# An LSTM's new cell moves from PSUM to SBUF, its forget gate from SBUF to PSUM

## The chip, the cores and the metric

One NeuronCore of one Trainium2 chip. The metric is the device time of one execution in microseconds; lower is better.

## What is computed

Sixteen sequences of 128 steps with 128 features pass through two LSTM layers that follow each other: the first feeds an attention without softmax, the second a feed-forward block, each with a residual. The recurrence is what matters here:

```
def step(carry, xp_t):
    prev_h, prev_c = carry
    h_bar = xp_t + prev_h @ Wh
    i = sigmoid(h_bar[:, 0:H]);      f = sigmoid(h_bar[:, H:2*H])
    o = sigmoid(h_bar[:, 2*H:3*H]);  g = tanh(h_bar[:, 3*H:4*H])
    next_c = f * prev_c + i * g
    next_h = o * tanh(next_c)
...
x = x + attn(lstm1(x, cond), W_theta, W_phi, W_g)    # attn: (theta phi^T / sqrt(128)) g
x = x + relu(lstm2(x, cond) @ W1 + b1) @ W2 + b2
```

The hidden size H is 128, so `Wh` is 128 x 512. There are 2 x 128 = 256 steps, each needs the one before it, and the second layer can't begin before the first has ended.

## The kernel before

The hidden state lies transposed, features on the 128 partitions and the 16 batch rows as columns, so that everything in a step is 128 x 16. `ring` keeps h of 16 steps in fp32; `h_hi` and `h_lo` keep it split into two fp16 numbers. A layer is cut into chunks of 8 steps (`CH`); ITER loops of 16 steps (`STEPS`) run over a layer. The first loop and, for layer 1, the last are written out, the others are hardware loops.

Each engine runs its own list in order, and the engines are tied together by semaphores set by hand. In a step:

- TensorE (`step`, L408): waits for `ring` and multiplies it by `whf`, the forget gate's fp32 weights (L420), into `fbank`; then `h_hi` and `h_lo` by the fp16 weights of g and i (L414) into `gibank`, then by those of o into `bankV`. After that it does what stands beside the step (`beside1` for layer 1: projections, attention, transposes; feed-forward products and projections for layer 2) and filler matmuls (`keep_warm`, L389, and `add_zeros`, L400), some of which wait for the o gate's sigmoid.
- ScalarE (ACT, L787): forget sigmoid from `fbank` to `fgate` (L795); one tanh for i and g together, from `gibank` into slots of `scan` (L802; sigmoid is had from tanh of the half, which is why the cell is kept at a doubled scale); o's sigmoid to `ogate` (L806); the tanh of the new cell to `tanhc` (L809). Copies such as `seed_o` (L825) stand between steps.
- VectorE (DVE, L983): the forget product `fgate` times old cell into every third column of `scan` (L987); `tensor_tensor_scan` over 48 columns (L990), which does the multiply and add for each of 16 batch rows in three columns and leaves the new cell in each third column; `ogate_h` (L995); `ring`, the new h in fp32 (L998), `h_hi` (L1000) and `h_lo` (L1003).

`cell` is a PSUM bank. Its first 48 columns are the scan's output `c_scan`, the next 16 are `tanhc`; `c_psum` is every third column of `c_scan`. `fgate`, `ogate`, `ogate_h` and `scan` are in SBUF. At the very end the bank `cell` also takes one product of the feed-forward block.

Of the kernel before, what the change touches and what calls it, by code (L numbers as in the profile page):

```python
# [30 lines left out]
def build(nc, x, cond, l1_wx, l1_wh, l1_b, w_theta, w_phi, w_g,  # L31
# [5 lines left out]
    ACT = mybir.ActivationFunctionType  # L37

    NB, T, D = x.shape
    H = D  # L40
    LAT = w_theta.shape[0]
    P = 128
# [19 lines left out]
    with ctx:  # L62
        def sb(name, shape, dt=f32):
            return ctx.enter_context(nc.sbuf_tensor(name, shape, dt))

        def ps(name):
            return ctx.enter_context(nc.psum_tensor(name, [P, 512], f32))

        def sem(name):
            return ctx.enter_context(nc.semaphore(name))  # L70
# [34 lines left out]
        w2 = sb("w2", [P, NJ, D])  # L105
        b1 = sb("b1", [P, NJ])
        b2 = sb("b2", [P, D])
        fgate = sb("fgate", [P, NB])
        ogate = sb("ogate", [P, NB])
        scan = sb("scan", [P, 98])  # L110

        h_hi = sb("h_hi", [P, STEPS, NB], f16)
        h_lo = sb("h_lo", [P, STEPS, NB], f16)
# [25 lines left out]
        fbank = [ps("fbank0"), ps("fbank1")]  # L139
        cell = ps("cell")  # L140
        bankU, bankV, bankY = ps("bankU"), ps("bankV"), ps("bankY")
        c_scan, tanhc = cell[:, 0:3 * NB], cell[:, 3 * NB:4 * NB]
        c_psum = c_scan.rearrange("p (b k) -> p b k", k=3)[:, :, 2]
        scan_mul, scan_add = scan[:, 0:3 * NB], scan[:, 3 * NB + 1:6 * NB + 1]
        gi_slots = scan[:, 2:6 * NB + 2].rearrange("p (g b k) -> p g b k", g=2, k=3)[:, :, :, 0]
        fc_slots = scan_add.rearrange("p (b k) -> p b k", k=3)[:, :, 2]
# [39 lines left out]
        hi_ready = [sem("hi_ready1"), sem("hi_ready2")]  # L186
# [60 lines left out]
        def rest_of_first(g):  # L247

            nc.vector.scalar_tensor_tensor(out=part(0, 1, g), in0=wh[0][:, gate_cols(g)], scalar=w_unit(0),
                                           in1=part(0, 0, g), op0=ALU.mult, op1=ALU.subtract  # L250
                                           ).then_inc(parts_ready[0], 1)
# [489 lines left out]
        def _(act):  # L741
# [9 lines left out]
            def high_parts(layer):  # L751

                nc.scalar.mul(wh_parts[layer][:, 0, :], wh[layer][:], w_unit(layer)).then_inc(parts_ready[layer], 1)
# [33 lines left out]
            def step(layer, s, n, first=False, opening=False):  # L787

                p, t = s // CH, s % CH
                n1 = n + 1  # L790
                if opening:
                    act.sem_inc(f_done[layer], 1)
                else:
                    act.wait_ge(f_ready[layer], n1)
                    nc.scalar.activation(fgate[:], fbank[p][:, NB * t:NB * t + NB],  # L795
                                         ACT.Sigmoid, scale=1.0 / Z_UNIT).then_inc(f_done[layer], 1)
                if first:
                    act.wait_ge(wh_ready, 1)
                    act.wait_ge(scale_made[0], SCALED - 2)
                    high_parts(0)  # L800
                act.wait_ge(gi_ready[layer], n1)
                nc.scalar.activation(gi_slots,  # L802
                                     gibank[p][:, 2 * NB * t:2 * NB * (t + 1)].rearrange("p (g b) -> p g b", g=2),
                                     ACT.Tanh, scale=0.5 / Z_UNIT).then_inc(scan_inputs[layer], 1)
                act.wait_ge(o_ready[layer], n1)
                nc.scalar.activation(ogate[:], bankV[:, (2 + p) * P + NB * t:(2 + p) * P + NB * t + NB],  # L806
                                     ACT.Sigmoid, scale=1.0 / Z_UNIT).then_inc(o_done[layer], 1)
                act.wait_ge(c_ready[layer], n1)
                nc.scalar.activation(tanhc, c_psum, ACT.Tanh,  # L809
                                     scale=0.5).then_inc(h_inputs[layer], 1)  # L810

            def keep_rows(slot, i, c, bank=bankY):
# [38 lines left out]
            for s in range(STEPS):  # L851
                step(0, s, s, first=s == 0, opening=s == 0)
                beside1(0, s, first=True)
                if s < 2:
                    keep_proj(s)
                set_layer2(s)
            with act.Fori(1, ITER - 1) as i:
                for s in range(STEPS):
                    step(0, s, i * STEPS + s)
                    beside1(i, s)  # L860
            for s in range(STEPS):
                step(0, s, (ITER - 1) * STEPS + s)
                beside1(ITER - 1, s, last=s >= CH)
# [29 lines left out]
        def _(dve):  # L893
# [89 lines left out]
            def step(layer, s, n, first=False, opening=False):  # L983
                n1 = n + 1
                if not opening:
                    dve.wait_ge(f_done[layer], n1)
                    nc.vector.tensor_tensor(out=fc_slots, in0=fgate[:], in1=c_psum,  # L987
                                            op=ALU.mult).then_inc(scan_inputs[layer], 1)
                dve.wait_ge(scan_inputs[layer], n * 2 + 2)
                nc.vector.tensor_tensor_scan(out=c_scan, data0=scan_mul, data1=scan_add, initial=0.0,  # L990
                                             op0=ALU.mult, op1=ALU.add).then_inc(c_ready[layer], 1)
                if first:
                    rest_of_first(GI)
                dve.wait_ge(o_done[layer], n1)
                nc.vector.tensor_tensor(out=ogate_h[:], in0=ogate[:], in1=unit_fill[layer][:],  # L995
                                        op=ALU.mult).then_inc(h_inputs[layer], 1)
                dve.wait_ge(h_inputs[layer], n * 2 + 2)
                nc.vector.tensor_tensor(out=ring[:, s, :], in0=tanhc, in1=ogate_h[:],  # L998
                                        op=ALU.mult).then_inc(h_ready[layer], 1)
                nc.vector.tensor_tensor(out=h_hi[:, s, :], in0=tanhc, in1=ogate_h[:],  # L1000
                                        op=ALU.mult).then_inc(hi_ready[layer], 1)
                dve.wait_ge(hi_ready[layer], n1)
                nc.vector.tensor_tensor(out=h_lo[:, s, :], in0=ring[:, s, :], in1=h_hi[:, s, :],  # L1003
                                        op=ALU.subtract).then_inc(lo_ready[layer], 1)
                if first:
                    rest_of_first(GO)
# [34 lines left out]
            for s in range(STEPS):  # L1041
                step(0, s, s, first=s == 0, opening=s == 0)
                beside1(0, s)
                if s == 1:
                    most_of(w_halves[:, 0:1], slice(0, 2 * H), 1, wh2_loaded)
                if s == 2:
                    most_of(w_halves[:, 1:2], slice(2 * H, 4 * H), 1, wh2_loaded)
                if s == 3:
                    dve.wait_ge(scale_made[1], 2)
                    nc.vector.tensor_reduce(w_most[1][:], w_halves[:], axis=mybir.AxisListType.X, op=ALU.max  # L1050
                                            ).then_inc(scale_made[1], 1)
                    spread_most(1, 3)
                if s == 4:
                    top_of(1, bankU[:, 2 * P:3 * P])
                if s == 6:
                    power_of(1, 5)
                if s == 7:
                    inverse_of(1, 7)
                if s == 8:
                    units_of(1, 8)  # L1060
                if s == 9:
                    fills_of(1, 10)
                if s == 14:
                    rest_of_second(slice(0, H))
                if s == 15:
                    rest_of_second(slice(2 * H, 4 * H))
            with dve.Fori(1, ITER) as i:
                for s in range(STEPS):
                    step(0, s, i * STEPS + s)
                    beside1(i, s)  # L1070
# [48 lines left out]
            with dve.Fori(1, ITER) as i:  # L1119
                for s in range(STEPS):  # L1120
                    p, t = s // CH, s % CH
# [44 lines left out]
```

## Time and profile before

| | |
|---|---|
| median of 3 runs | 435.31 us (435.3 to 435.46) |
| span of the profiled execution | 431.1 us |
| PE, matmul | 413.9 us busy, 96% |
| PE, weight load | 301.4 us, 70% |
| DVE | 282.0 us, 65% |
| ACT | 192.1 us, 45% |
| granted TensorE clock | full through the whole span |

The profiled execution's own time isn't given apart from its span; the median of the runs lies 4.2 us above the span. PE is busy time of matmuls, whose ends are modelled since they are pipelined, and PEld is the weight load that overlaps them. A high busy share of an engine doesn't say that the engine sets the time: the waits, and the timeline of one step, do.

### The profile page before, as it was taken

The page shows a single profiled execution, that of the slowest core. Times are in us where ns is not written, and L with a number is a line of the kernel's source. Part 1 is how long each engine was busy: PE and PEld are TensorE (multiplying, and loading weights), DVE is VectorE, ACT ScalarE, POOL GpSimd, SP SyncE. Part 2 cuts the span into 40 slices and gives each one's busy share as a digit, 9 for nine tenths or more (in the row PEclk, how much of TensorE's full clock was granted, in tenths as well). Part 3 has the DMA queues.
Part 4 walks back from the last instruction along what each step waited for, and adds up shares of the span by engine and source line. Part 5 has one row for each costly group of instructions (what it writes and reads, how often), then busy time and mean ns, then how long its engine had stood idle before and what let it go on. Part 6 is the DMA issues. An engine that isn't in the chain of part 4 may idle for free.

```text
span 431.1 us, 14329 instructions
## 1 busy us (share of the span) xinstructions
PE 413.9 (96%) x5020; PEld 301.4 (70%) x5020; DVE 282.0 (65%) x1702; ACT 192.1 (45%) x1132; POOL 7.8 (2%) x20
## 2 busy tenths in 40 slices
PE   8999999999999999999999999999999999999996
PEld 5767666666766666666689777777777777777775
DVE  6766666666666666666668766666667666666664
ACT  3565444445444444544445433343443434343342
POOL 7000000000000000000000000000000000000000
PEclk9999999999999999999999999999999999999999
DMA  5011011111001111000000100000000000000000
GB/s 180 10 20 20 13 10 18 18 18 18 13 5 18 18 18 18 16 2 14 14 14 2 27 21 6 12 18 20 18 18 0 18 18 18 18 17 1 18 18 12
DMA packets 11694, 8.19 MB, mean 19 GB/s; under 512 B 1097, under 2 KB 11129, under 8 KB 11674
## 3 DMA queue, kind: packets, MB, share of 16 engines
q1 hardware_dynamic: 10874, 6.17, 7.2%
q0 software_dynamic: 512, 1.22, 0.9%
q10 hardware_dynamic: 288, 0.52, 0.4%
q8 instruction: 13, 0.21, 0.2%
q14 instruction: 7, 0.06, 0.0%
HBM read 2.87 MB, written 1.05 MB: 9 GB/s over the span
## 4 chain that ended last, share of the span: by engine, by line
PE 83%; ACT 7%; DVE 5%; issue 3%; DMA 1%; SPq 0%; DVEq 0%
PE fbank L420 19%; PE bankV L400 14%; PE gibank L414 9%; PE bankU L389 6%; PE bankV L414 5%; PE gibank L377 4%; PE bankY L619 4%; PE bankU L612 3%; DVE cell L990 3%; PE bankV L484 3%; ACT scan L802 3%; PE bankY L479 2%; ACT fgate L795 2%; PE gibank L383 2%; PE bankU L512 2%
## 5 line engine op out<-in xcount | busy, mean ns | idle before, releaser
L420 PEld LDWEIGHTS fbank<-ring,whf 128*128 128x128 f32 x508 | 76.6, 188 | 91.7 <-DVE ring L998 88.1
L795 ACT ACTIVATE fgate<-fbank 128x16 f32<-128x16 f32 x254 | 46.5, 183 | 153.5 <-PE fbank L420 153.2
L420 PE MATMUL fbank<-ring,whf 128*128 128x16 f32 x508 | 98.2, 269 | 6.1 <-DVE ring L998 0.7
L987 DVE TENSOR_TENSOR scan<-fgate,cell 128x16 f32<-128x16 f32 x254 | 45.1, 178 | 77.5 <-ACT fgate L795 75.4
L400 PE MATMUL bankV<-warm_x,zeros 128*128 128x512 bf16 x294 | 93.0, 379 | 0.0
L990 DVE TENSOR_TENSOR_SCAN cell<-scan 128x48 f32<-128x48 f32 x256 | 68.2, 267 | 12.0 <-ACT scan L802 1.1
L809 ACT ACTIVATE cell<-cell 128x16 f32<-128x16 f32 x256 | 43.0, 168 | 67.9 <-DVE cell L990 67.8
L998 DVE TENSOR_TENSOR ring<-cell,ogate_h 128x16 f32<-128x16 f32 x256 | 44.7, 174 | 41.8 <-ACT cell L809 41.6
L414 PEld LDWEIGHTS gibank<-h_hi,wh_parts 128*128 128x128 f16 x1016 | 65.4, 117 | 0.0
L414 PE MATMUL gibank<-h_hi,wh_parts 128*128 128x16 f16 x1016 | 62.1, 169 | 0.0
L414 PE MATMUL gibank<-h_lo,wh_parts 128*128 128x16 f16 x1016 | 62.0, 169 | 0.0
L802 ACT ACTIVATE scan<-gibank 128x32 f32<-128x32 f32 x256 | 54.5, 213 | 4.2 <-PE gibank L383 1.6
L1003 DVE TENSOR_TENSOR h_lo<-ring,h_hi 128x16 f16<-128x16 f32 x256 | 44.9, 175 | 8.7
L414 PE MATMUL bankV<-h_hi,wh_parts 128*128 128x16 f16 x508 | 49.3, 169 | 0.0
L414 PE MATMUL bankV<-h_lo,wh_parts 128*128 128x16 f16 x508 | 49.3, 169 | 0.0
L806 ACT ACTIVATE ogate<-bankV 128x16 f32<-128x16 f32 x256 | 46.9, 183 | 0.0
L414 PEld LDWEIGHTS gibank<-h_lo,wh_parts 128*128 128x128 f16 x1016 | 43.4, 96 | 0.0
L1000 DVE TENSOR_TENSOR h_hi<-cell,ogate_h 128x16 f16<-128x16 f32 x256 | 42.1, 165 | 0.0
L995 DVE TENSOR_TENSOR ogate_h<-ogate,unit_fill 128x16 f32<-128x16 f32 x256 | 41.5, 162 | 0.0
L389 PE MATMUL bankU<-warm_x,warm_w 128*128 128x512 bf16 x128 | 37.9, 377 | 0.0
L400 PEld LDWEIGHTS bankV<-warm_x,zeros 128*128 128x128 bf16 x294 | 29.0, 99 | 8.7
L414 PEld LDWEIGHTS bankV<-h_lo,wh_parts 128*128 128x128 f16 x508 | 30.6, 96 | 0.0
(182 smaller groups left out, 505.6 us busy)
## 6 DMA issues: line engine op xcount, KB each, us to landing
rows_t<-rows SPq DMA_DIRECT2D x16, 128.0 KB
x_rows<-in_x_dram SPq DMA_DIRECT2D x17, 64.0 KB
out_dram<-y_sb SPq DMA_DIRECT2D x16, 64.0 KB
xres<-x2T SPq DMA_DIRECT2D x15, 64.0 KB, 1.9
xin<-x2T SPq DMA_DIRECT2D x14, 64.0 KB, 1.9
w<-in_L_ffn_W_dram POOLq DMA_DIRECT2D x2, 256.0 KB, 4.1
wh<-in_L_cond_Wh_dram ACTq DMA_DIRECT2D x1, 256.0 KB, 2.7
wx<-in_L_cond_Wx_dram ACTq DMA_DIRECT2D x1, 256.0 KB, 3.6
```

The lines of the kernel that those rows point to most:

```text
L389: nc.tensor.matmul(bank[:, :], warm_w[:], warm_x[:], start=True, stop=True)
L400: nc.tensor.matmul(bankV[:, :], zeros[:, 0:P], warm_x[:], start=False, stop=True, skip_group_check=True)
L414: last = nc.tensor.matmul(step_out(p, t, g), wh_parts[layer][:, part, gate_cols(g)], h[:, (s - 1) % STEPS, :], start=False, stop=True, ski ...
L420: nc.tensor.matmul(step_out(p, t, GF), whf[layer][:], ring[:, (s - 1) % STEPS, :], start=False, stop=True, skip_group_check=True).then_inc ...
L795: nc.scalar.activation(fgate[:], fbank[p][:, NB * t:NB * t + NB], ACT.Sigmoid, scale=1.0 / Z_UNIT).then_inc(f_done[layer], 1)
L802: nc.scalar.activation(gi_slots, gibank[p][:, 2 * NB * t:2 * NB * (t + 1)].rearrange("p (g b) -> p g b", g=2), ACT.Tanh, scale=0.5 / Z_UNI ...
L806: nc.scalar.activation(ogate[:], bankV[:, (2 + p) * P + NB * t:(2 + p) * P + NB * t + NB], ACT.Sigmoid, scale=1.0 / Z_UNIT).then_inc(o_don ...
L809: nc.scalar.activation(tanhc, c_psum, ACT.Tanh, scale=0.5).then_inc(h_inputs[layer], 1)
L987: nc.vector.tensor_tensor(out=fc_slots, in0=fgate[:], in1=c_psum, op=ALU.mult).then_inc(scan_inputs[layer], 1)
L990: nc.vector.tensor_tensor_scan(out=c_scan, data0=scan_mul, data1=scan_add, initial=0.0, op0=ALU.mult, op1=ALU.add).then_inc(c_ready[layer], 1)
L998: nc.vector.tensor_tensor(out=ring[:, s, :], in0=tanhc, in1=ogate_h[:], op=ALU.mult).then_inc(h_ready[layer], 1)
L1003: nc.vector.tensor_tensor(out=h_lo[:, s, :], in0=ring[:, s, :], in1=h_hi[:, s, :], op=ALU.subtract).then_inc(lo_ready[layer], 1)
```

## The change

The scan's output `c_scan` becomes an SBUF tensor of its own, [128, 48] in fp32; the new cell, every third column of it, is called `c_new`. `fgate` leaves SBUF and takes the first 16 columns of the PSUM bank `cell`; `tanhc` follows it in columns 16 to 31. The instructions are the same, in the same order. ACT gets one wait more: before the forget sigmoid of step n it waits until `hi_ready` has reached n, which is when DVE has made `h_hi` of the step before, the last reader of `tanhc` in the bank that the sigmoid now writes.

```diff
-        fgate = sb("fgate", [P, NB])
         ogate = sb("ogate", [P, NB])
         scan = sb("scan", [P, 98])
+        c_scan = sb("c_scan", [P, 3 * NB])
...
-        c_scan, tanhc = cell[:, 0:3 * NB], cell[:, 3 * NB:4 * NB]
-        c_psum = c_scan.rearrange("p (b k) -> p b k", k=3)[:, :, 2]
+        fgate, tanhc = cell[:, 0:NB], cell[:, NB:2 * NB]
+        c_new = c_scan[:].rearrange("p (b k) -> p b k", k=3)[:, :, 2]
...
                 else:
+                    act.wait_ge(hi_ready[layer], n)
                     act.wait_ge(f_ready[layer], n1)
-                    nc.scalar.activation(fgate[:], fbank[p][:, NB * t:NB * t + NB],
+                    nc.scalar.activation(fgate, fbank[p][:, NB * t:NB * t + NB],
                                          ACT.Sigmoid, scale=1.0 / Z_UNIT).then_inc(f_done[layer], 1)
...
-                nc.scalar.activation(tanhc, c_psum, ACT.Tanh,
+                nc.scalar.activation(tanhc, c_new, ACT.Tanh,
                                      scale=0.5).then_inc(h_inputs[layer], 1)
...
-                    nc.vector.tensor_tensor(out=fc_slots, in0=fgate[:], in1=c_psum,
+                    nc.vector.tensor_tensor(out=fc_slots, in0=fgate, in1=c_new,
                                             op=ALU.mult).then_inc(scan_inputs[layer], 1)
                 dve.wait_ge(scan_inputs[layer], n * 2 + 2)
-                nc.vector.tensor_tensor_scan(out=c_scan, data0=scan_mul, data1=scan_add, initial=0.0,
+                nc.vector.tensor_tensor_scan(out=c_scan[:], data0=scan_mul, data1=scan_add, initial=0.0,
                                              op0=ALU.mult, op1=ALU.add).then_inc(c_ready[layer], 1)
```

## Rows read from the trace of the kernel before

**Rows 1.** The page: busy time by engine, and the chain that ended last

```profile
PE 413.9 (96%) x5020; PEld 301.4 (70%) x5020; DVE 282.0 (65%) x1702; ACT 192.1 (45%) x1132; POOL 7.8 (2%) x20
...
PE 83%; ACT 7%; DVE 5%; issue 3%; DMA 1%; SPq 0%; DVEq 0%
```

**Rows 2.** Waits: engine and line, for whom; us in total, times, longest

```profile
PEld fbank L420 <- DVE ring L998: 88.1, 226, 0.5
```

**Rows 3.** Timeline, one step of layer 1: start us, length us, instruction

```profile
105.86 0.38 PE L400 MATMUL bankV<-warm_x,zeros 128*128 128x512 bf16 x1
105.95 0.17 DVE L998 TENSOR_TENSOR ring<-cell,ogate_h 128x16 f32<-128x16 f32 x1 [0.16 <-ACT cell L809]
106.05 0.17 DVE L1000 TENSOR_TENSOR h_hi<-cell,ogate_h 128x16 f16<-128x16 f32 x1
106.18 0.30 PEld L420 LDWEIGHTS fbank<-ring,whf 128*128 128x128 f32 x2 [0.44 <-DVE ring L998]
...
106.61 0.18 ACT L795 ACTIVATE fgate<-fbank 128x16 f32<-128x16 f32 x1 [0.69 <-PE fbank L420]
...
106.81 0.21 ACT L802 ACTIVATE scan<-gibank 128x32 f32<-128x32 f32 x1
106.83 0.18 DVE L987 TENSOR_TENSOR scan<-fgate,cell 128x16 f32<-128x16 f32 x1 [0.41 <-ACT fgate L795]
...
107.05 0.27 DVE L990 TENSOR_TENSOR_SCAN cell<-scan 128x48 f32<-128x48 f32 x1
...
107.23 0.16 DVE L995 TENSOR_TENSOR ogate_h<-ogate,unit_fill 128x16 f32<-128x16 f32 x1
107.35 0.17 ACT L809 ACTIVATE cell<-cell 128x16 f32<-128x16 f32 x1 [0.26 <-DVE cell L990]
...
107.55 0.17 DVE L998 TENSOR_TENSOR ring<-cell,ogate_h 128x16 f32<-128x16 f32 x1 [0.16 <-ACT cell L809]
```

**Rows 4.** Groups by line and form, ACT: busy us, mean ns | idle before

```profile
L802 ACT ACTIVATE scan<-gibank 128x32 f32<-128x32 f32 x256 | 54.5, 213 | 4.2 <-PE gibank L383 1.6
...
L795 ACT ACTIVATE fgate<-fbank 128x16 f32<-128x16 f32 x254 | 46.5, 183 | 153.5 <-PE fbank L420 153.2
L809 ACT ACTIVATE cell<-cell 128x16 f32<-128x16 f32 x256 | 43.0, 168 | 67.9 <-DVE cell L990 67.8
L825 ACT COPY bankV<-o_bias 128x128 f32<-128x128 f32 x31 | 8.2, 264 | 0.0
...
L839 ACT ACTIVATE xT<-bankU 128x128 f32 x12 | 3.3, 277 | 0.2
...
L771 ACT ACTIVATE wx<-wx 128x128 f32<-128x128 f32 x1 | 0.3, 302 | 0.0
...
L821 ACT COPY o_bias<-bankV 128x128 f32<-128x128 f32 x1 | 0.3, 265 | 0.2 <-PE bankV L377 0.2
```

**Rows 5.** Timeline of ACT, second step of layer 1, sigmoid held up

```profile
12.00 0.20 ACT L795 ACTIVATE fgate<-fbank 128x16 f32<-128x16 f32 x1
12.09 0.21 ACT L802 ACTIVATE scan<-gibank 128x32 f32<-128x32 f32 x1
```

**Rows 6.** Groups by line and form, DVE

```profile
L990 DVE TENSOR_TENSOR_SCAN cell<-scan 128x48 f32<-128x48 f32 x256 | 68.2, 267 | 12.0 <-ACT scan L802 1.1
...
L1003 DVE TENSOR_TENSOR h_lo<-ring,h_hi 128x16 f16<-128x16 f32 x256 | 44.9, 175 | 8.7
L998 DVE TENSOR_TENSOR ring<-cell,ogate_h 128x16 f32<-128x16 f32 x256 | 44.7, 174 | 41.8 <-ACT cell L809 41.6
...
L995 DVE TENSOR_TENSOR ogate_h<-ogate,unit_fill 128x16 f32<-128x16 f32 x256 | 41.5, 162 | 0.0
...
L1135 DVE TENSOR_TENSOR y_sb<-bankY,b 128x128 f32<-128x128 f32 x14 | 4.0, 287 | 0.0
```

**Rows 7.** Timeline, a step of layer 2 with late TensorE: filler, sigmoid

```profile
307.18 0.81 PE L400 MATMUL bankV<-warm_x,zeros 128*128 128x512 bf16 x3
...
308.15 0.18 ACT L795 ACTIVATE fgate<-fbank 128x16 f32<-128x16 f32 x1 [0.93 <-PE fbank L420]
```

## The prediction

> **What bounds the kernel now.** I read the busy shares first. TensorE shows 96% of the span, and the chain that ended last gives PE 83% [rows 1], which looks like a kernel bound by TensorE. It isn't: much of that work is filler (the products of `warm_x`), and the wait list says who waits for whom. The weight load of the forget gate's matmul sat idle for DVE's `ring` 226 times, 88.1 us in all, 0.39 us a time [rows 2]. So in 226 of the 256 steps TensorE has caught up and waits for the recurrence.
>
> Next the timeline of one step [rows 3]. From `ring` at 105.95 to the next at 107.55 is 1.60 us, and 256 steps of it are 410 of the 431.1 us of the span. Its links, start to start: `ring` to the load of `whf` 0.23, to the forget sigmoid 0.43, to the i/g tanh 0.20, to the scan 0.24, to the cell tanh 0.30, to `ring` 0.20. A nanosecond on one of these links in every step is worth about 0.23 us.
>
> **What changes in a step.** Four instructions get other operands: the forget sigmoid writes PSUM, the forget product (L987) has `fgate` as its PSUM operand and no longer the cell, the scan writes SBUF, the cell tanh reads SBUF. ACT gets one more wait. No DMA and no matmul is touched.
>
> **Forget sigmoid: worth nothing.** On ACT the write to PSUM is the cheaper one: the sigmoid to SBUF is 183 ns, the cell tanh, PSUM to PSUM at the same width, 168 [rows 4]. The sigmoid should fall by 15 ns, or by up to 25 (the tanh has a stride, below). But nobody waits for it last. The i/g tanh starts 0.20 us after it [rows 3], and could start sooner: in a step where its input had long been there it started 0.09 us after the sigmoid, at 12.09 after 12.00 [rows 5]. In the ordinary step TensorE's i/g products set its start. The product L987 does follow the sigmoid, but it ends at 106.83 + 0.18 = 107.01, the i/g tanh at 106.81 + 0.213 = 107.023, and the scan starts 0.027 later [rows 3, 4]. So the i/g tanh is last, and the sigmoid's gain is hidden behind it: 0. It can't turn into a cost, since the product only gets more lead.
>
> **Forget product: 0.** It had one operand in PSUM and has one after, so its 0.18 us [rows 3] should stay. A growth of some ns is covered by its earlier start.
>
> **Cell tanh: +24 ns, on the path.** SBUF to PSUM at this width isn't in the trace. Two ways lead to it. First, wide activations: PSUM to SBUF is 277 ns (L839), SBUF to SBUF 302 (L771) [rows 4], so reading SBUF costs 25 more; 168 + 25 = 193. Second, wide copies: SBUF to PSUM (L825) is 264, PSUM to SBUF (L821) 265 [rows 4], so the direction makes no difference and the tanh would cost what the sigmoid costs, 183. But this one reads with a stride of three. The i/g tanh writes with that stride: 213 ns for 32 elements, where 183 + 16 x 0.84 = 196 would be due (0.84 = (277 - 183)/112 [rows 4]), so the stride costs some 0.5 ns an element, 8 ns for 16; 183 + 8 = 191. I take 192, +24. Bounds: +15 (stride free) and +38 (each strided read costs a second element's time, 25 + 13). Below zero it can't go unless SBUF is read faster than PSUM, and 302 against 277 excludes that.
>
> **Scan: -12 ns, on the path.** No DVE instruction but the scan writes PSUM. The nearest row is the price of reading PSUM: `ring`, with one PSUM operand, is 174 ns, `ogate_h`, the same product all in SBUF, 162 [rows 6]. That is 12 ns for the crossing, and I take the write to cost the same; on ACT, read and write cost alike (264 against 265). The bounds come from splitting its 267 ns [rows 6]. An element costs DVE 1.0 ns ((287 - 174)/112, `y_sb` against `ring`), so an all-SBUF product has a fixed part of 146 (`ogate_h`: 162 - 16) to 159 ns (`h_lo`: 175 - 16) [rows 6]. If the scan takes one such time an element, 48 ns, 219 are fixed and the write to PSUM costs 60 to 73. If it takes two (a multiply and an add that need the last result), 171 are fixed and the write costs 12 to 25. At the other end the write costs nothing. I take 12: the nearest row, and the low end of the two-time case.
>
> The Trainium skill says (DVE: opcode table, instruction layouts, handler registers and perf-mode slots, section Datapath and trigger behaviour) that the built-in scan runs at half throughput, which is the two-time case; no row here shows it. By that page the write would cost 12 to 25 ns and the sum would still end at slower or about the same.
>
> **The added wait: 0.** ACT now waits for `hi_ready` of the step before, ahead of `f_ready`. Behind it on ACT are the forget sigmoid and the rest of that step's activations. `h_hi` ends at 106.05 + 0.17 = 106.22 and the sigmoid starts at 106.61 [rows 3]: 0.39 us of cover, in which ACT is idle. Without that cover each nanosecond would count 226 times.
>
> **Sum.** 24 - 12 = 12 ns a step. It counts in the 226 steps in which TensorE waits for `ring`; in the other 30 something else is late and takes 12 ns without notice. 226 x 12 = 2.7 us: the span goes from 431.1 to 433.8. The median of the runs, 435.31, lies 4.2 above the profiled span; with the same 4.2 the time is 438.0 us.
>
> **The rivals.**
> (a) The forecast, slower by 0.2 to 1% (net +4 to +19 ns): 438.0 us. For it: the ACT price rests on two ways that agree within 2 ns. Against it: the scan's price is borrowed from a read. Chance 0.47.
> (b) Faster: the scan's write to PSUM is dear, 60 to 73 ns. Net -36 to -49, times 226 is -8.1 to -11.1 us, so 425.7 us. The sign turns as soon as the write costs more than the tanh's 24. Nothing would be in the way of such a gain: `ogate_h` ends at 107.39, 0.16 us before `ring` starts, and the filler ahead of the forget matmul ends at 106.24, 0.37 before the sigmoid [rows 3], where elsewhere a filler that ended at 307.99 let the sigmoid start 0.16 later [rows 7]. Against it: reading PSUM costs DVE only 12 ns. Chance 0.16. A mild form, write 28 to 39 ns, gives 431.9 to 434.4 us; chance 0.06.
> The Trainium skill leans to this side (VectorE: DVE Perf Modes, section on the TRN2 errata): it gives VectorE a fixed 58 cycles with an SBUF source and 120 with a PSUM source, ScalarE 224 and 172. Carried over to this swap, -65 and +43 ns a step would be an estimate of about 430 us. The trace disagrees on both sizes for reads, 12 and 25 ns.
> (c) The two cancel within 4 ns, say tanh +20, scan -20: 435.3 us. Chance 0.14.
> (d) Slower by more: the strided read from SBUF costs ACT +38, the scan gains 12; 26 x 226 = 5.9, so 441.2 us. Chance 0.13.
> (e) The wait: if what ACT's sequencer does behind it takes more than 0.39 us, the sigmoid comes late. At 40 ns too much, with the +12, 52 x 226 = 11.8 us, so 447.1 us. Against it: the size of the cover. Chance 0.04.
>
> **How the numbers follow.** A measurement of this kernel can tell about 0.2% from no change, 0.9 us, so 4 ns a step. Slower: (a), (d), (e) = 0.64. Same: (c) = 0.14. Faster: (b) and its mild form = 0.22. The range takes in (a), (c), (d) and the mild form and leaves out the dear write and (e), 0.20: from 431.9 (net -15) to 442.1 (net +30). The cases in it have both signs; (a) alone would be 436.2 to 439.6.
>
> **What the profile after would show.** Cell tanh 192 ns (183 means that the stride is free, over 205 is (d)). Scan 255 ns (194 to 207 is (b)). Forget sigmoid 158 to 168, the i/g tanh still 0.20 us behind it; if that distance moved with the sigmoid, TensorE doesn't pace it. Sigmoid still 0.43 us after the load; longer is (e). A step of 1.61 us. The prediction is wrong at its core if the scan loses more than the tanh gains.

## The result: 1.5% slower, and the profile after

The changed kernel takes 441.8 us, median of 4 runs, against 435.31: a ratio of 1.0149, 95% interval 1.0116 to 1.0182. In a second set of runs on another chip it was 442.5 us and 1.0132 (1.0086 to 1.0178). So it is slower by about 6.5 us where 2.7 were forecast. A ratio is taken over the fast executions alone, so it isn't quite the quotient of the two medians.

The profiled span is 439.9 us. Its own execution took 441.98 us, so that 2.1 us lie outside of the span. That corrects a term of the prediction: the span of 431.1 us belonged to an execution of about 433.2 us (an estimate), not to one of 435.31. The difference of the two spans, 8.8 us, is therefore larger than that of the medians, and both the start-up and the clock (below) have a part in it.

The groups of ACT and DVE, in the form of [rows 4, 6] (line, engine, operation, operands, count | busy us, mean ns | idle before):

```profile
L796 ACT ACTIVATE cell<-fbank 128x16 f32<-128x16 f32 x254 | 42.7, 168 | 157.2 <-PE fbank L420 156.9
L988 DVE TENSOR_TENSOR scan<-cell,c_scan 128x16 f32<-128x16 f32 x254 | 45.7, 180 | 78.5 <-ACT cell L796 76.1
L810 ACT ACTIVATE cell<-c_scan 128x16 f32<-128x16 f32 x256 | 50.0, 195 | 67.6 <-DVE c_scan L991 67.4
L999 DVE TENSOR_TENSOR ring<-cell,ogate_h 128x16 f32<-128x16 f32 x256 | 44.7, 175 | 49.7 <-ACT cell L810 49.7
L991 DVE TENSOR_TENSOR_SCAN c_scan<-scan 128x48 f32<-128x48 f32 x256 | 65.9, 257 | 13.8 <-ACT scan L803 1.0
...
L803 ACT ACTIVATE scan<-gibank 128x32 f32<-128x32 f32 x256 | 54.8, 214 | 6.8 <-PE gibank L383 1.6
...
L996 DVE TENSOR_TENSOR ogate_h<-ogate,unit_fill 128x16 f32<-128x16 f32 x256 | 38.3, 150 | 0.0
```

The cell tanh (now L810) went from 168 to 195 ns, the scan (L991) from 267 to 257, the forget sigmoid (L796) from 183 to 168. On the path the first two count: +27 - 10 = +17 ns a step by their lengths.

A step inside the hardware loops, from the timeline (start us, length us), against [rows 3]:

```profile
303.52 0.17 DVE L999 TENSOR_TENSOR ring<-cell,ogate_h 128x16 f32<-128x16 f32 x1 [0.19 <-ACT cell L810]
303.61 0.16 DVE L1001 TENSOR_TENSOR h_hi<-cell,ogate_h 128x16 f16<-128x16 f32 x1
303.75 0.30 PEld L420 LDWEIGHTS fbank<-ring,whf 128*128 128x128 f32 x2 [0.23 <-DVE ring L999]
304.18 0.17 ACT L796 ACTIVATE cell<-fbank 128x16 f32<-128x16 f32 x1 [0.51 <-PE fbank L420]
304.37 0.22 ACT L803 ACTIVATE scan<-gibank 128x32 f32<-128x32 f32 x1
304.38 0.18 DVE L988 TENSOR_TENSOR scan<-cell,c_scan 128x16 f32<-128x16 f32 x1 [0.40 <-ACT cell L796]
304.62 0.26 DVE L991 TENSOR_TENSOR_SCAN c_scan<-scan 128x48 f32<-128x48 f32 x1
...
304.91 0.19 ACT L810 ACTIVATE cell<-c_scan 128x16 f32<-128x16 f32 x1 [0.25 <-DVE c_scan L991]
```

The links are those of before, 0.23, 0.43, 0.19, 0.25, but for scan to tanh (0.29) and tanh to `ring` (0.23). The median of all looped steps goes from 1.60 to 1.62 us, 19 to 21 ns more according to which of two profiles of the kernel before is taken; 152 of the 208 take 1.62 us. A step of the code that is written out (the first 16 steps of each layer and the last 16 of layer 1, 46 steps with a forget sigmoid) looks otherwise:

```profile
196.45 0.17 DVE L999 TENSOR_TENSOR ring<-cell,ogate_h 128x16 f32<-128x16 f32 x1 [0.20 <-ACT cell L810]
196.54 0.16 DVE L1001 TENSOR_TENSOR h_hi<-cell,ogate_h 128x16 f16<-128x16 f32 x1
196.68 0.30 PEld L420 LDWEIGHTS fbank<-ring,whf 128*128 128x128 f32 x2 [0.38 <-DVE ring L999]
197.17 0.17 ACT L796 ACTIVATE cell<-fbank 128x16 f32<-128x16 f32 x1 [0.45 <-PE fbank L420]
197.31 0.21 ACT L803 ACTIVATE scan<-gibank 128x32 f32<-128x32 f32 x1
197.37 0.18 DVE L988 TENSOR_TENSOR scan<-cell,c_scan 128x16 f32<-128x16 f32 x1 [0.46 <-ACT cell L796]
197.59 0.26 DVE L991 TENSOR_TENSOR_SCAN c_scan<-scan 128x48 f32<-128x48 f32 x1
...
198.10 0.17 DVE L999 TENSOR_TENSOR ring<-cell,ogate_h 128x16 f32<-128x16 f32 x1 [0.19 <-ACT cell L810]
```

The sigmoid starts 0.49 us after the load, not 0.43. The i/g tanh isn't moved (196.68 + 0.63, as ever), but the forget product now ends at 197.55, after the i/g tanh at 197.52, and it starts the scan. The step takes 1.65 to 1.66 us. Six steps inside the loops are late in the same way, 1.65 us with the sigmoid at 0.49: the last one of each of the six rounds of layer 1's loop.

With that the difference of the two profiled executions can be laid out, by the starts of `ring` in the timelines:

| stretch | before, us | changed, us | difference |
|---|---|---|---|
| start to the first `ring` | 9.57 | 10.19 | +0.6 |
| next 15 steps, written out | 24.20 | 25.25 | +1.1 |
| 96 looped steps of layer 1 | 153.96 | 156.04 | +2.1 |
| 12 written-out steps | 19.31 | 19.92 | +0.6 |
| 4 steps up to the change of layer | 6.40 | 7.90 | +1.5 |
| 16 steps from there on | 28.56 | 29.66 | +1.1 |
| 112 looped steps of layer 2 | 183.12 | 185.00 | +1.9 |

The four steps stand out; they run from 211.4 to 219.3 us. The windows over them (start:end, length, busy us by engine, then the granted clock) show TensorE falling to half of its clock, 1.2 GHz in place of 2.4. Before the fall it was busy for 3.54 of 4.00 us:

```profile
208.00:212.00 4.00, 3.54 (x46) 2.61 (x45) 2.30 (x15) 2.08 (x12) 0.00 (x0) 1.00 0.10 24
212.00:214.00 2.00, 2.00 (x29) 1.36 (x26) 0.93 (x6) 0.62 (x5) 0.00 (x0) 0.83 0.13 27
214.00:216.00 2.00, 2.00 (x14) 1.08 (x12) 1.28 (x7) 0.62 (x4) 0.00 (x0) 0.50 0.00 0
216.00:220.00 4.00, 4.00 (x34) 2.57 (x35) 2.09 (x13) 1.25 (x8) 0.00 (x0) 0.50 0.00 0
```

The step behind them, the opening one of layer 2, still begins at half clock. It takes 4.28 us, 0.5 us more than in the other profile of the changed kernel.

### The profile page after: what moved, and what is told of

Its sections match the earlier page's. It is cut to its first block, busy times and chain, and to the rows that moved or that the text cites. A ratio compares the mean times of both kernels' runs of the same rounds, so it can differ in the third digit from the quotient of the medians.

```text
span 439.9 us, 14394 instructions
## 1 busy us (share of the span) xinstructions
PE 419.7 (95%) x5020; PEld 303.0 (69%) x5020; DVE 279.2 (63%) x1702; ACT 194.1 (44%) x1132; POOL 7.8 (2%) x20
## 4 chain that ended last, share of the span: by engine, by line
PE 76%; DVE 11%; ACT 7%; issue 4%; DMA 1%; DVEq 0%; ACTq 0%
PE fbank L420 19%; PE bankV L400 13%; PE gibank L414 10%; DVE c_scan L991 4%; PE gibank L377 4%; PE bankV L414 4%; PE bankY L619 4%; PE bankU L612 3%; ACT cell L810 3%; DVE ring L999 3%; PE bankV L484 3%; PE bankU L389 3%; ACT scan L803 3%; PE bankY L479 2%; PE gibank L383 2%
## 5 line engine op out<-in xcount | busy, mean ns | idle before, releaser
L420 PEld LDWEIGHTS fbank<-ring,whf 128*128 128x128 f32 x508 | 77.5, 189 | 97.7 <-DVE ring L999 94.1
L796 ACT ACTIVATE cell<-fbank 128x16 f32<-128x16 f32 x254 | 42.7, 168 | 157.2 <-PE fbank L420 156.9
L988 DVE TENSOR_TENSOR scan<-cell,c_scan 128x16 f32<-128x16 f32 x254 | 45.7, 180 | 78.5 <-ACT cell L796 76.1
L810 ACT ACTIVATE cell<-c_scan 128x16 f32<-128x16 f32 x256 | 50.0, 195 | 67.6 <-DVE c_scan L991 67.4
L991 DVE TENSOR_TENSOR_SCAN c_scan<-scan 128x48 f32<-128x48 f32 x256 | 65.9, 257 | 13.8 <-ACT scan L803 1.0
L389 PE MATMUL bankU<-warm_x,warm_w 128*128 128x512 bf16 x128 | 39.4, 390 | 0.0
L996 DVE TENSOR_TENSOR ogate_h<-ogate,unit_fill 128x16 f32<-128x16 f32 x256 | 38.3, 150 | 0.0
L414 PEld LDWEIGHTS bankV<-h_hi,wh_parts 128*128 128x128 f16 x508 | 30.6, 96 | 0.0
```

What stands on the lines that cost most here:

```text
L389: nc.tensor.matmul(bank[:, :], warm_w[:], warm_x[:], start=True, stop=True)
L414: last = nc.tensor.matmul(step_out(p, t, g), wh_parts[layer][:, part, gate_cols(g)], h[:, (s - 1) % STEPS, :], start=False, stop=True, ski ...
L420: nc.tensor.matmul(step_out(p, t, GF), whf[layer][:], ring[:, (s - 1) % STEPS, :], start=False, stop=True, skip_group_check=True).then_inc ...
L796: nc.scalar.activation(fgate, fbank[p][:, NB * t:NB * t + NB], ACT.Sigmoid, scale=1.0 / Z_UNIT).then_inc(f_done[layer], 1)
L810: nc.scalar.activation(tanhc, c_new, ACT.Tanh, scale=0.5).then_inc(h_inputs[layer], 1)
L988: nc.vector.tensor_tensor(out=fc_slots, in0=fgate, in1=c_new, op=ALU.mult).then_inc(scan_inputs[layer], 1)
```

## Why the sigmoid is late: the list of instructions

The list of the built program (no time in it) shows what became of the two waits. An instruction carries one wait; a second becomes an instruction of its own. Which one depends on the order in the source and on what stands ahead. ACT, written-out code, before and changed, then the looped code of the changed kernel:

```
Activation      waits f_ready1  >= 113     signals f_done1

EventSemaphore  waits f_ready1  >= 113
Activation      waits hi_ready1 >= 112     signals f_done1

RegisterAlu add waits hi_ready1 >= register
Activation      waits f_ready1  >= register   signals f_done1
```

The wait written last, on the semaphore that comes late, was put on an instruction ahead of the sigmoid, and the one that had long been met rides on the sigmoid. In the loops an addition to a register stands there anyway and took the early wait. I counted 46 written-out steps with the late wait apart. The trace of the changed kernel has 52, the other six being those in the loops (L795 is the line of the wait; count, length in ns, first and last start in us):

```profile
L795 ACTq ALU_OP  x202: 35/35/49, 35.7 to 432.6; - x101
L795 ACTq EVENT_SEMAPHORE  x52: 17/17/17, 10.9 to 248.0; - x52
```

Theory: the first form costs 60 ns at the sigmoid wherever it stands. Rivals: the sigmoid is late because it writes the bank that DVE has just read, or because code that isn't looped has more instructions to fetch. The experiments below separate this from the price of the operands.

## Experiments

**The two waits in the other order.** Nothing else is touched.

```diff
-                    act.wait_ge(hi_ready[layer], n)
                     act.wait_ge(f_ready[layer], n1)
+                    act.wait_ge(hi_ready[layer], n)
```

> The changed kernel with the two waits ahead of the forget sigmoid in the other order: f_ready first, hi_ready second. Built, the wait written first rides on the sigmoid itself and the second becomes an instruction of its own in the steps that are written out; here that is hi_ready, which is there 0.3 us early. Theory (a wait of its own on f_ready makes the sigmoid 60 ns late in the 46 written-out steps, and the longer steps let the granted TensorE clock fall between the layers): the sigmoid starts 0.43 us after the weight load in all steps, the written-out steps take 1.62 us and not 1.66, the clock stays full, the time is about 439.4 us. Rival (the sigmoid is late there because it writes the bank that DVE has just read, or because there are more instructions to fetch): it stays at 0.49 us and the time at 441.8. Second rival (the clock falls for a reason of its own): 0.43 us, but a half-speed stretch remains and the time is about 440.7.

Measured 439.28 us, ratio to before 1.0107 (1.0021 to 1.0194); this chip scattered more than the first. The trace is clearer than the time. A step of written-out code:

```profile
196.04 0.17 DVE L999 TENSOR_TENSOR ring<-cell,ogate_h 128x16 f32<-128x16 f32 x1 [0.20 <-ACT cell L810]
196.27 0.30 PEld L420 LDWEIGHTS fbank<-ring,whf 128*128 128x128 f32 x2 [0.35 <-DVE ring L999]
196.70 0.17 ACT L796 ACTIVATE cell<-fbank 128x16 f32<-128x16 f32 x1 [0.39 <-PE fbank L420]
196.89 0.21 ACT L803 ACTIVATE scan<-gibank 128x32 f32<-128x32 f32 x1
...
197.66 0.17 DVE L999 TENSOR_TENSOR ring<-cell,ogate_h 128x16 f32<-128x16 f32 x1 [0.19 <-ACT cell L810]
```

The sigmoid is back at 0.43 us and the step at 1.62, though it still writes the same bank and the written-out code has just as many instructions. Both rivals fall. The wait's own instruction starts at 196.32 in this step, 0.38 us ahead of the sigmoid; in the changed kernel's step at 196.45 it starts at 197.11, 0.06 us ahead. The clock stayed full in this profiled execution, but not in others (below), so that part of the theory isn't shown.

**The wait alone, in the order of the change, added to the kernel before.**

```diff
+                    act.wait_ge(hi_ready[layer], n)
                     act.wait_ge(f_ready[layer], n1)
```

> The kernel before with only the added wait, in the order of the changed kernel; no operand is moved. Theory: the written-out steps get the sigmoid at 0.49 us and take about 1.66 us, 46 x 0.05 = 2.4 us, and if the clock falls as well 1.5 to 2 us more: 437.7 to 439.7 us. The looped steps stay at 1.60 us. Rival (the wait is free and the late sigmoid belongs to the PSUM write): 435.3 us and 0.43 us everywhere.

Measured 438.94 us, ratio 1.0061 (1.0024 to 1.0099). Written-out steps:

```profile
196.09 0.30 PEld L420 LDWEIGHTS fbank<-ring,whf 128*128 128x128 f32 x2 [0.33 <-DVE ring L999]
196.58 0.18 ACT L796 ACTIVATE fgate<-fbank 128x16 f32<-128x16 f32 x1 [0.58 <-PE fbank L420]
```

0.49 us again with no operand moved, steps of 1.65 us, and looped steps at 1.60 but for the same six. The wait has its own price, about 0.6%. Here the written-out step is 50 ns longer than the looped one, in the changed kernel only some 35 ns: there the sigmoid to PSUM is 15 ns shorter, and in these steps that does count.

**The wait alone, in the other order.**

```diff
                     act.wait_ge(f_ready[layer], n1)
+                    act.wait_ge(hi_ready[layer], n)
```

> The kernel before with the added wait alone, but with f_ready written first and hi_ready second. Theory (the wait is free as long as the late semaphore rides on the sigmoid): sigmoid at 0.43 us in written-out and looped steps, all steps 1.60 us, 435.3 us, no difference from before. Rival (any added instruction costs in the written-out steps): sigmoid later than 0.43 us there, 436 to 438 us.

Measured 436.17 us, ratio 1.0002 (0.9967 to 1.0038), sigmoid at 0.43 to 0.44 us and steps of 1.60 us in written-out and looped code alike. The interval overlaps that of the other order, so the times alone don't tell the two apart. The traces do: 47 late steps, all but those of the start-up and of the half clock, are 2.2 us shorter in this order. The wait is free as long as the late semaphore rides on the sigmoid, with one exception, in the ninth step of layer 1. There ACT copies the output gate's bias just ahead of the sigmoid. Before:

```profile
21.19 0.30 PEld L420 LDWEIGHTS fbank<-ring,whf 128*128 128x128 f32 x2
21.41 0.27 ACT L821 COPY o_bias<-bankU 128x128 f32<-128x128 f32 x1 [0.48 <-PE bankU L553]
21.62 0.18 ACT L795 ACTIVATE fgate<-fbank 128x16 f32<-128x16 f32 x1
```

With the wait in this order:

```profile
24.38 0.30 PEld L420 LDWEIGHTS fbank<-ring,whf 128*128 128x128 f32 x2
24.61 0.27 ACT L822 COPY o_bias<-bankU 128x128 f32<-128x128 f32 x1 [0.49 <-PE bankU L553]
25.00 0.18 ACT L796 ACTIVATE fgate<-fbank 128x16 f32<-128x16 f32 x1
```

The sigmoid no longer starts while the copy runs but 0.13 us after its end, 0.62 us after the load, and the step takes 1.78 us. In the changed kernel it is 0.82 us after the load and the step takes 1.98. All six profiles with the added wait have a long step here, 1.76 us or more; the two of the kernel before and that of the cell alone have 1.60 to 1.62.

**The cell alone to SBUF.** The forget gate stays in SBUF, and no wait is needed.

```diff
+        c_scan = sb("c_scan", [P, 3 * NB])
...
-        c_scan, tanhc = cell[:, 0:3 * NB], cell[:, 3 * NB:4 * NB]
-        c_psum = c_scan.rearrange("p (b k) -> p b k", k=3)[:, :, 2]
+        tanhc = cell[:, 3 * NB:4 * NB]
+        c_new = c_scan[:].rearrange("p (b k) -> p b k", k=3)[:, :, 2]
```

> Half of the change: the scan writes SBUF and the tanh reads it there; the forget gate stays in SBUF, no wait is added. Theory (scan -10, tanh +27, nothing else on the path): looped and written-out steps both at 1.62 us, clock full, 435.3 + 226 x 0.017 = 439.2 us; the forget product, all in SBUF, falls to about 167 ns and gains nothing. Rival (the forget product's or the sigmoid's time counts after all): under 438.5 us, and the scan starts less than 0.24 us after the i/g tanh.

Measured 440.6 us, ratio 1.0100 (1.0065 to 1.0135); steps of 1.62 us in loops and written-out code alike, the scan 0.24 to 0.25 us after the i/g tanh. The steps are as expected, the clock isn't: it fell between the layers in this profile, and the median is 1.4 us above the 439.2 that I expected. The groups:

```profile
L810 ACT ACTIVATE cell<-c_scan 128x16 f32<-128x16 f32 x256 | 49.9, 195 | 65.5 <-DVE c_scan L991 65.4
...
L796 ACT ACTIVATE fgate<-fbank 128x16 f32<-128x16 f32 x254 | 46.5, 183 | 153.6 <-PE fbank L421 153.4
...
L991 DVE TENSOR_TENSOR_SCAN c_scan<-scan 128x48 f32<-128x48 f32 x256 | 65.9, 257 | 11.0 <-ACT scan L803 1.1
L988 DVE TENSOR_TENSOR scan<-fgate,c_scan 128x16 f32<-128x16 f32 x254 | 46.5, 183 | 79.9 <-ACT fgate L796 77.7
```

This half gives the whole growth of the looped step. With a sigmoid of 183 ns it has the same step as the swapped kernel with 168, so the sigmoid's 15 ns are worth nothing there. My 167 ns for a forget product all in SBUF was wrong: it takes 183, longer than with a PSUM operand (178).

**Two probes of stride and length.** In each the scan covers 24 of its 48 columns and the tanh reads 16 columns in a row; half of the cell isn't computed. First with the cell in SBUF, then in the kernel before, with it in PSUM.

```diff
-                nc.scalar.activation(tanhc, c_new, ACT.Tanh,
+                nc.scalar.activation(tanhc, c_scan[:, 0:NB], ACT.Tanh,
...
-                nc.vector.tensor_tensor_scan(out=c_scan[:], data0=scan_mul, data1=scan_add, initial=0.0,
+                nc.vector.tensor_tensor_scan(out=c_scan[:, 0:24], data0=scan_mul[:, 0:24], data1=scan_add[:, 0:24], initial=0.0,
```

> As the half change with the cell in SBUF, but the scan runs over 24 of the 48 columns and the tanh reads the first 16 columns in a row, not every third; the cell is cleared once at the start. Half of the cell is not computed. Scan 257 ns before the cut: 207 ns if an element takes two DVE times, 232 if one. Tanh 195 ns strided: 187 ns if the stride costs 0.5 ns an element, 195 if it is free.

```profile
L810 ACT ACTIVATE cell<-c_scan 128x16 f32<-128x16 f32 x256 | 48.0, 187 | 53.1 <-DVE c_scan L992 52.8
...
L992 DVE TENSOR_TENSOR_SCAN c_scan<-scan 128x24 f32<-128x24 f32 x256 | 53.1, 207 | 10.9 <-ACT scan L803 1.1
```

> The two cuts of the SBUF probe in the kernel before, with the cell in PSUM: the scan runs over 24 of 48 columns, the tanh reads 16 columns in a row; half of the cell is not computed. Scan 267 ns before the cut: 217 ns if an element takes two times, 242 if one. Tanh 168 ns strided: 158 to 160 if the stride costs 0.5 ns an element in PSUM too, 168 if it is free.

```profile
L809 ACT ACTIVATE cell<-cell 128x16 f32<-128x16 f32 x256 | 43.0, 168 | 54.6 <-DVE cell L991 54.5
...
L991 DVE TENSOR_TENSOR_SCAN cell<-scan 128x24 f32<-128x24 f32 x256 | 55.4, 216 | 12.2 <-ACT scan L802 1.1
```

24 columns fewer take off 50 ns in SBUF and 51 in PSUM: 2.1 ns an element, two of DVE's element times. The two probes ran once each, 425.22 and 423.82 us; as they leave out work, only the lengths of the instructions are used. They settle the split of the scan's 267 ns: 100 for elements, and 9 to 10 for writing PSUM in place of SBUF, at either length. The rival with a dear write is dead. The Trainium skill says of the built-in scan that it runs at half throughput (DVE: opcode table, instruction layouts, handler registers and perf-mode slots, section Datapath and trigger behaviour); these two runs agree.

The tanh: in SBUF the stride costs 195 - 187 = 8 ns, in PSUM nothing (168 both ways). So its +27 are 19 for reading SBUF and 8 for the stride.

**The changed kernel and the swapped one on one chip**, with more rounds.

> The changed kernel as it is, on the chip and in the rounds of the two waits beside it. Looped steps 1.62 us, written-out steps 1.655 with the sigmoid 0.49 us after the load; about 441.5 us. What is new to learn is how much it moves from run to run: where the kernel before scatters by several us on a chip, so should this one.

> The changed kernel with the two waits in the other order, again, on the same chip as the changed kernel itself. Theory (46 written-out steps are 35 ns shorter): 1.6 us less than the changed kernel, about 439.7 us, and 1.0% over the kernel before. Rival (the order of the waits shows in the trace but not in the time, since something else is late): no difference.

Measured: changed 442.5 us, ratio 1.0132 (1.0086 to 1.0178); swapped 439.84 us, 1.0096 (1.0059 to 1.0134). The order of the waits is worth 2.7 us between the medians. The intervals overlap, so the time alone doesn't prove it. The traces do. Without those at half clock, the late steps are 1.8 us shorter in all in the swapped kernel, most of them by 30 to 40 ns, the ninth by 0.22 us. The changed kernel scattered less than I had expected, 440.7 to 442.72 us in 6 runs where the kernel before went from 433.27 to 441.06 in 23.

**The kernel before, profiled again.**

> The kernel before, nothing changed, for a second profile. Its profiled span was 431.1 us, while on another chip its spans lay at 433.2 in most runs. Theory: the 256 steps are the same 1.60 us and what differs lies in the first fifteen steps, where DMAs are late or not, and in the four steps between the layers, where the granted TensorE clock falls in some runs. Rival: the steps themselves differ from run to run.

Span 433.4 us. From the first `ring` on, the stretches of the table are 25.15 (before 24.20), 153.86, 19.31, 6.40, 28.54 and 182.98 us: the steps repeat to 0.1%. The first `ring` starts at 11.26 us against 9.57. The waits of the start-up show part of it as a DMA that came later, here:

```profile
ACT wh_parts L753 <- DVE scale L950: 3.6, 1, 3.6
DVE bias L963 <- DMA bias<-in_L_cond_b_dram: 2.2, 1, 2.2
```

In the first profile these were 2.4 and 1.5 us. So the 2.3 us between two profiles of one kernel lie in its first 15 steps and ahead of them. The clock was full in both. It fell between the layers in the profiles of the changed kernel, of the wait alone in the change's order, of the cell alone and of the swapped kernel's second run, where the four steps took 1.0, 1.1 and 2.0 us more than before in the last three, and it is under 1.000 in many runs of the kernel before too. What sets it off isn't shown. It needs neither the added wait nor the late order, since it fell without them. But of the 20 executions with the waits in the change's order none had a full mean clock, of the kernel before 10 of 42 and of the other three variants 14 of 38 (0.999 or more); so the late order may make a fall likelier, which no run here settles.

## Why the prediction was right in kind and short in size

*The bound (the recurrence, not TensorE): right.* What scan and tanh lost came back in full in the looped step: 17 ns by their lengths, 18 by their links in the timeline (-8 and +26), 19 to 21 in the step.

*Forget sigmoid 0: right where it isn't late.* It fell by 15 ns, and the cell-only kernel, without that, has the same step. In the late steps it hides 15 of the 60 ns of lateness.

*Forget product 0: right*, 178 to 180 ns, covered.

*Cell tanh +24: right in mechanism, 3 ns short* (+27). One of the two ways, 168 + 25, took it that the 168 already held the stride. In PSUM the stride is free; reading SBUF costs 19 at this width, not 25, and the stride 8. The other way, 183 + 8, had the stride right and was 4 short. That the two ways agreed within 2 ns was luck: their errors are of different kinds.

*Scan -12: right in mechanism, 2 ns too much* (-10). That the borrowed price of a read came so near was luck. It was 174 - 162, `ring` against `ogate_h`, and `ogate_h` turned out to depend on what the scan ahead of it writes (below): in the changed kernel the same pair is 175 and 150, 25 ns apart. Against `h_lo`, also all in SBUF (175), it would have been nothing.

*Steps that count, 226: nearly right.* Set side by side, from the shorter of two profiles of each kernel, 236 of the 255 distances from `ring` to `ring` are at least 10 ns longer in the swapped kernel than before. Of the others 13 are the steps of layer 2's loops in which TensorE runs late (1.83 and 1.89 us in both). The other 30 of the wait list were those in which the load wasn't seen idle; in some of them `ring` sets its start all the same. The sum is 4.6 us, of which 0.16 are the ninth step; that leaves some 4.5 us for the operands, 236 x 19, in place of 226 x 12 = 2.7. The swapped and the cell-only kernels, at 1.0096 to 1.0107, give 4.2 to 4.7.

*The added wait 0: the step that failed.* I asked whether `hi_ready` comes in time, and it does, by 0.39 us. I didn't ask on which instruction each wait would come to lie. In 52 steps the late semaphore, `f_ready`, moved off the sigmoid, which then starts 60 ns later; the product's lead and the shorter sigmoid take up some of it, and some 35 ns are left. With the 0.22 us that the ninth step loses by the late order that is 1.8 us, and 0.16 us come from the wait itself in that step: 2.0 us where I had put 0. Rival (e) had the right place at ACT. Its cause was wrong, since the cover of 0.39 us was enough, and its total far too high: its 40 ns a step were of the right order, but they were to count in 226 steps.

*Together* 4.5 + 2.0 = 6.5 us, as measured; the interval of the ratio is 5.0 to 7.9 us. That it comes out so close is partly luck, as start-up and clock move single executions by 1 to 2 us. The forecast of 438.0 us was low by its tanh and scan (5 ns a step by their lengths, 7 to 9 in the step itself) and by the wait, in about equal parts. The sum was also set against the wrong time outside of the span (4.2 us, where 2.1 is right); as the same amount was taken off and put back, that cost nothing.

The Trainium skill's fixed costs (VectorE: DVE Perf Modes, section on the TRN2 errata) would have made the change faster, by an estimated 22 ns a step. The runs gave 9 to 10 ns for the scan's write and 19 for ACT's read, where the differences worked out from its figures, an estimate, are 65 and 43 ns.

## What to carry to other kernels

In a recurrence that waits link by link, price a moved operand on each engine that touches it: here the scan gains 10 ns, the tanh loses 27, and the sigmoid's 15 lie off the path. When an instruction gets a second wait, see to it that the semaphore that comes last stays on the instruction itself; look at the built list, in loops and in written-out code apart. Count the steps in which a thing happens in the trace, not from the source alone: the late wait stood in 52 steps, where the written-out code has 46.

## What the runs showed of the hardware that I had not expected

A wait for a late semaphore in an instruction of its own on ACT costs 60 ns from semaphore to sigmoid over the same wait on the sigmoid (0.49 against 0.43 us after the load). Behind a copy, even a wait that had long been met, in an instruction of its own, made the sigmoid start 0.19 us later (0.62 against 0.43 us).

An instruction's length can depend on what the one ahead of it reads or writes. `ogate_h`, all in SBUF and itself unchanged, fell from 162 to 150 ns once the scan ahead of it wrote SBUF. The copy of the bias seeds right after the cell tanh fell from 264 to 250 ns once that tanh read SBUF; in the kernel with only the cell moved:

```profile
L826 ACT COPY bankV<-o_bias 128x128 f32<-128x128 f32 x31 | 7.8, 250 | 0.0
```

Neither is on the path. A DVE product with both inputs in SBUF, one of them strided, takes 183 ns, against 178 with the strided one in PSUM; that the stride is the cause is my guess, no run here separates it.
